# A macaron block with a spiking feed-forward: the first batch loaded and normalised in pieces, the last tiles' sums woven

## The chip, the cores and the metric

One core of a Trainium2 chip runs the whole program. The metric is the device time in microseconds of one execution; lower is better. Three runs of the kernel before gave 158.92 us in the median (158.81 to 158.99).

## What is computed

```python
x = x + 0.5 * ffn(layernorm(x), W_fc, W_proj)
x = x + attention(layernorm(x))
x = x + 0.5 * ffn(layernorm(x), W_fc, W_proj)

def ffn(x, W_fc, W_proj):                 # x: 8 batches, 512 tokens, 128 features; float32
    h = square(relu(x @ W_fc.T))          # 512 hidden features
    y = h @ W_proj.T
    # 5 steps of a leaky integrate-and-fire neuron driven by y: the number of spikes / 5
def attention(h):
    keys, values = h @ Wk.T + bk, h @ Wv.T + bv
    w = exp((keys @ Wka.T + bka) / sqrt(128))
    return cumsum(w / cumsum(w) * keys) * values
```

## The kernel before

The work is 16 feed-forward jobs (two layers of 8 batches) and 8 attention jobs in one software pipeline. Every engine runs the same loop over steps i from -3 to 18 and in each step issues its share of job i, of the jobs ahead (i+1, i+2) and behind (i-1, i-2, i-3); the order within a step is written out by hand, and semaphores tie the engines together. A batch is 512 tokens by 128 features, held as four tiles of 128 tokens (NT = 4). The eight PSUM banks are hidden[0] to hidden[3], work[0] and work[1] (one for each of two lanes, odd and even jobs), att_work and att_value.

A feed-forward job goes like this. VectorE takes BN_STATS and BN_AGGR of each tile (L488, L491) and reduces to var + eps and -mean (L497, L499); GpSimd raises var + eps to -0.5 (L330) and normalises four tiles (L338). TensorE turns them (transposes with the identity, L725) into work[lane]; ScalarE copies the bank to in_hi in the reduced float format of the matmul (L385), VectorE subtracts it from the bank to get the rest, in_lo (L522). An expand (L713, L714, L717) is three matmuls in one bank: fc_lo with in_hi, fc_hi with in_hi, fc_hi with in_lo; there are four, one for each 128 hidden features, and the first waits for in_lo only before its third matmul. ScalarE takes the relu (L389), squares are shared among ScalarE, VectorE and GpSimd, and four contracts (L760) sum y in work[lane]. The spikes are counted by comparing y with levels.

The first job differs: VectorE normalises it (first_normalise, L516), after GpSimd's inverse deviation alone. Its order on VectorE in step -1 is layer_norm of all four tiles, the cast of the identity to 16 bits (L622), first_normalise, then fc_low_part (L626), which makes fc_lo for all 512 columns from hidden[2], where the turned fc weights stand, and ScalarE's fc_hi (L448). In step 0 comes in_lo. TensorE starts with 14 transposes of the identity into hidden[0], results unused (fillers, L837), turns the fc weights (L840) and the projection weights (L844), issues 8 fillers (L847), turns the batch, issues 10 fillers (L867) and, after a wait for fc_lo, starts the first expand. ScalarE copies the turned projection weights (L450) right behind fc_hi.

SyncE issues the loads in this order: batch 0 as one load of 256 KB (L301), the projection weights (L302), batch 1, three attention weights, batch 2, five vectors, batches 3 to 7. ScalarE issues the fc weights (L381).

The last job ends tile by tile: TensorE contracts tile t into a bank of its own (L770, y_tiles) over hidden chunks c = 1 to 3, all three of tile 0 first, then of tile 1, and so on (chunk 0 of all tiles goes before; the matmul of one tile and chunk shows as two passes). ScalarE makes three 128-column steps of each tile (stairs, L403). VectorE (last_tiles) adds them in two operations (L541, L546) and adds the residual in a third (L550), each waiting for the one before, tile after tile. SyncE stores each tile (L316). Chunks 1 and 2 of the last job's squares are VectorE's (L534), 3 is ScalarE's.

Of the kernel before, what the change touches and what calls it, by code (L numbers as in the profile page):

```python
# [146 lines left out]
def macaron_kernel(nc, x, wk, bk, wka, bka, wv, bv, gamma, beta, w_fc, w_proj, out):  # L147
# [4 lines left out]
    HALF = S // 2  # L152
# [13 lines left out]
    WARM_UP, WARM_UP_TURN, WARM_UP_FIRST = 14, 8, 10  # L166
# [7 lines left out]
    with ExitStack() as ctx:  # L174
# [18 lines left out]
        att_work, att_value = bank("att_work"), bank("att_value")  # L193
        last_lane = (len(FF_JOBS) - 1) % 2
# [57 lines left out]
        x_loaded = [sem(f"x_loaded{b}") for b in range(NB)]  # L252
# [25 lines left out]
        sum_tile_made, x_tile_made = sem("sum_tile_made"), sem("x_tile_made")  # L278
# [42 lines left out]
        def _(pool):  # L321
# [6 lines left out]
            def normalise(kind, turn, source, by_dve=False):  # L328
# [3 lines left out]
                if by_dve:  # L332
                    return
# [7 lines left out]
            def ff_normalise(j):  # L341
                normalise(j.lane, j.turn, x_of[j.layer][j.batch], by_dve=j.index == 0)
# [37 lines left out]
        def _(act):  # L380
            act.dma_start(fc_raw[:], w_fc.rearrange("(c p) d -> p c d", p=P)).then_inc(fc_loaded, 16)  # L381

            def ff_hi(j):
                act.wait_ge(turned[j.lane], j.turn + 1)
                nc.scalar.activation(in_hi[j.lane][:], work[j.lane][:], ACT.Copy).then_inc(hi_made[j.lane], 1)  # L385
# [63 lines left out]
            act.wait_ge(proj_turned, 1)  # L449
            nc.scalar.activation(flat(proj_t), att_value[:], ACT.Copy).then_inc(proj_ready, 1)  # L450

            for i in range(FIRST_STEP, STEPS):
# [25 lines left out]
                for j in feed_forward(i + 1):  # L478
                    ff_hi(j)
                for b in attention(i + 1):  # L480
                    att_part_hi(b)
# [3 lines left out]
        def _(dve):  # L485
# [15 lines left out]

            def ff_layer_norm(j):
# [10 lines left out]
            def first_normalise(j):  # L513
                dve.wait_ge(rstd_made[j.lane], 1)
                for t in range(NT):
# [20 lines left out]

            def last_tiles(j):
                for t in range(NT):
                    tokens = slice(t * P, (t + 1) * P)
                    dve.wait_ge(sign_tile_made, 3 * t + 2)  # L540
                    nc.vector.scalar_tensor_tensor(sign_sum[j.lane][:, tokens], stairs[j.lane][:, 0, tokens], 2.0,  # L541
                                                   stairs[j.lane][:, 1, tokens], ALU.min,
                                                   ALU.add).then_inc(sum_tile_made, 1)
                    dve.wait_ge(sign_tile_made, 3 * t + 3)
                    dve.wait_ge(sum_tile_made, 2 * t + 1)
                    nc.vector.scalar_tensor_tensor(sign_sum[j.lane][:, tokens], stairs[j.lane][:, 2, tokens], 2.0,  # L546
                                                   sign_sum[j.lane][:, tokens], ALU.min,
                                                   ALU.add).then_inc(sum_tile_made, 1)
                    dve.wait_ge(sum_tile_made, 2 * t + 2)
                    nc.vector.scalar_tensor_tensor(x_of["out"][j.batch][:, t, :], sign_sum[j.lane][:, tokens],  # L550
                                                   RESIDUAL_STEP, x_of["second"][j.batch][:, t, :], ALU.mult,
                                                   ALU.add).then_inc(x_tile_made, 1)
# [71 lines left out]
            def fc_low_part():  # L624
                dve.wait_ge(fc_hi_made, 1)
                nc.vector.tensor_tensor(flat(fc_lo), hidden[2][:], flat(fc_hi).bitcast(F32),  # L626
# [31 lines left out]
            for i in range(FIRST_STEP, STEPS):  # L658
# [40 lines left out]
                if i == -1:  # L699
                    fc_low_part()  # L700
# [9 lines left out]
        def _(pe):  # L710
# [8 lines left out]
            def ff_turn(j):  # L719
# [3 lines left out]
                for t in range(NT):  # L723
                    pe.wait_ge(normed_made[j.lane], NT * j.turn + t + 1)
                    last = nc.tensor.transpose(work[j.lane][:, t * P:(t + 1) * P], normed[j.lane][:, t, :], ident[:])  # L725
                last.then_inc(turned[j.lane], 1)

            def ff_expand(j, c):
                if c == 0:
# [45 lines left out]
            def last_contract_tiles(j):  # L775
                for t in range(NT):
                    for c in range(1, NC):
                        if t == 0:
                            wait_square(j, c)
                        last_contract(j, t, c)  # L780
# [61 lines left out]
            pe.wait_ge(proj_loaded, 16)  # L842
            for c in range(NC):
                last = nc.tensor.transpose(att_value[:, c * P:(c + 1) * P], proj_raw[:, c, :], ident[:])  # L844
            last.then_inc(proj_turned, 1)
# [3 lines left out]
            for i in range(FIRST_STEP, STEPS):  # L849
                for j in feed_forward(i):  # L850
                    ff_turn(j)
                for j in feed_forward(i - 1):
# [75 lines left out]
```

## Time and profile before

| | us |
|---|---|
| median of 3 runs | 158.92 |
| the profiled execution | 158.94 |
| its span, first to last instruction | 157.2 |

| engine | busy us | share of span |
|---|---|---|
| TensorE (PE) | 150.6 | 96% |
| VectorE (DVE) | 135.1 | 86% |
| ScalarE (ACT) | 122.0 | 78% |
| GpSimd (POOL) | 109.4 | 70% |

PE's row counts pipelined matmuls with modelled ends, so 96% is not an engine at its peak; PEld is the loading of weights, which overlaps it. In the timeline a row is a run of equal instructions: start, length of the run, engine, line, operation, what is written and read, how many, and in brackets the engine's idle time before it and what ended it. In the chain a row is a piece of the path that ended last: each piece goes back to what released it. SPq and ACTq are DMA issues. Times are from the start of the span.

### The profile page before, as it was taken

The numbers are of one execution on the slowest core, as the hardware profiler recorded it, in microseconds if no ns is written. First come the engines' busy times: TensorE is split into PE (matmuls) and PEld (weight loads), VectorE is DVE, ScalarE is ACT, GpSimd is POOL, SyncE is SP. The second block draws the span as 40 slices with busy tenths as digits, with TensorE's granted clock in tenths as the row PEclk, the third lists the DMA queues.
The fourth block names the chain that finished last, engine by engine and source line by source line (L and its number), as shares of the span: only waits on it lengthen the run. The fifth ranks groups of instructions, "written<-read, shape, count | busy, mean of one in ns | idle before, by whom it ended". The sixth has DMA issues, their size and how long they took to land.

```text
span 157.2 us, 2605 instructions
## 1 busy us (share of the span) xinstructions
PE 150.6 (96%) x783; PEld 104.5 (66%) x783; DVE 135.1 (86%) x391; ACT 122.0 (78%) x237; POOL 109.4 (70%) x165
## 2 busy tenths in 40 slices
PE   6999999999999999999999999999999999999980
PEld 6685747585767858668566785775866758564870
DVE  1685499798899999999999999999999999875864
ACT  3348798999997894968989789598696786987970
POOL 1219427999699878799899999999987569270200
PEclk9999999999999999999999999999999999999997
DMA  4991000000000000000000020000020201020221
GB/s 127 260 284 47 0 2 4 0 0 0 2 2 4 0 0 2 0 4 0 0 0 0 4 67 2 0 0 0 2 71 0 67 0 54 13 73 0 67 83 53
DMA packets 10334, 5.08 MB, mean 32 GB/s; under 512 B 1104, under 2 KB 10192, under 8 KB 10320
## 3 DMA queue, kind: packets, MB, share of 16 engines
q1 hardware_dynamic: 9792, 4.66, 10.2%
q10 hardware_dynamic: 528, 0.26, 0.6%
q8 instruction: 6, 0.10, 0.2%
q14 instruction: 8, 0.07, 0.1%
HBM read 2.82 MB, written 2.10 MB: 31 GB/s over the span
## 4 chain that ended last, share of the span: by engine, by line
PE 89%; DVE 4%; DMA 2%; ACT 2%; POOL 1%; issue 0%; DVEq 0%
PE work L760 33%; PE hidden L713 9%; PE hidden L717 9%; PE hidden L714 9%; PE hidden L798 6%; PE work L725 5%; PE att_work L713 2%; PE att_work L717 2%; PE att_work L714 2%; DMA x_first<-_attn_hidden_states_dram 2%; PE att_work L807 2%; PE att_value L831 2%; PE att_value L713 1%; PE att_value L717 1%; PE att_value L714 1%; ACT stairs L418 1%
## 5 line engine op out<-in xcount | busy, mean ns | idle before, releaser
L760 PE MATMUL work<-square,proj_t 128*128 128x512 f32 x120 | 58.0, 595 | 0.0
L389 ACT ACTIVATE relu<-hidden 128x512 f32<-128x512 f32 x64 | 39.6, 621 | 13.2 <-PE hidden L717 13.1
L422 ACT ACTIVATE signs<-work 128x512 bf16<-128x512 f32 x70 | 41.2, 609 | 7.2 <-PE work L760 7.2
L394 ACT ACTIVATE square<-relu 128x512 f32<-128x512 f32 x45 | 29.5, 655 | 0.6
L330 POOL TENSOR_TENSOR rstd<-var_eps,minus_half 128x4 f32<-128x4 f32 x16 | 17.2, 1077 | 17.6 <-DVE neg_mean L499 17.6
L760 PEld LDWEIGHTS work<-square,proj_t 128*128 128x128 f32 x120 | 20.3, 189 | 12.7 <-issue 6.0
L598 DVE RECIPROCAL inv_sum<-weight_sum 128x256 f32<-128x256 f32 x16 | 27.9, 1741 | 0.0
L713 PE MATMUL hidden<-in_hi,fc_lo 128*128 128x512 f32 x64 | 27.0, 422 | 0.0
L717 PE MATMUL hidden<-in_lo,fc_hi 128*128 128x512 f32 x64 | 25.3, 396 | 0.0
L714 PE MATMUL hidden<-in_hi,fc_hi 128*128 128x512 f32 x64 | 25.0, 391 | 0.0
L338 POOL TENSOR_SCALAR normed_att<-x_att,neg_mean_att,rstd_att 128x128 f32<-128x128 f32 x32 | 18.9, 605 | 0.8
L360 POOL TENSOR_TENSOR share<-weight,inv_sum 128x256 f32<-128x256 f32 x16 | 13.3, 831 | 5.7 <-DVE inv_sum L598 5.7
L338 POOL TENSOR_SCALAR normed<-x_second,neg_mean,rstd 128x128 f32<-128x128 f32 x32 | 16.4, 528 | 0.8
L350 POOL TENSOR_TENSOR square<-relu 128x512 f32<-128x512 f32 x10 | 10.4, 1045 | 8.0 <-ACT relu L389 8.0
L522 DVE TENSOR_TENSOR in_lo<-work,in_hi 128x512 fp32r<-128x512 f32 x16 | 11.0, 686 | 5.7 <-ACT in_hi L385 5.5
L717 PEld LDWEIGHTS hidden<-in_lo,fc_hi 128*128 128x128 f32 x64 | 12.0, 188 | 3.0 <-DVE in_lo L522 0.3
L725 PEld LDWEIGHTS work<-ident,normed 128*128 128x128 f32 x64 | 8.0, 140 | 8.9 <-ACT signs L422 4.1
L714 PEld LDWEIGHTS hidden<-in_hi,fc_hi 128*128 128x128 f32 x64 | 12.1, 189 | 2.2 <-issue 0.2
L713 PEld LDWEIGHTS hidden<-in_hi,fc_lo 128*128 128x128 f32 x64 | 12.1, 188 | 2.1 <-issue 0.2
L338 POOL TENSOR_SCALAR normed<-x_first,neg_mean,rstd 128x128 f32<-128x128 f32 x28 | 12.8, 472 | 0.7
L798 PEld LDWEIGHTS hidden<-ident,signs 128*128 128x128 bf16 x160 | 9.6, 98 | 4.6 <-issue 4.6
L363 POOL TENSOR_TENSOR share_key<-share,key 128x256 f32<-128x256 f32 x16 | 11.7, 730 | 1.3
(103 smaller groups left out, 262.9 us busy)
## 6 DMA issues: line engine op xcount, KB each, us to landing
x_first<-_attn_hidden_states_dram SPq DMA_DIRECT2D x8, 256.0 KB, 4.0
out_dram<-x_out SPq DMA_DIRECT2D x7, 256.0 KB, 2.2
fc_raw<-in_L_ffn_W_fc_dram ACTq DMA_DIRECT2D x1, 256.0 KB, 4.1
proj_raw<-in_L_ffn_W_proj_dram SPq DMA_DIRECT2D x1, 256.0 KB, 4.2
out_dram<-x_out SPq DMA_DIRECT2D x4, 64.0 KB, 1.5
att_raw<-in_L_attn_Wk_dram SPq DMA_DIRECT2D x1, 64.0 KB, 3.9
att_raw<-in_L_attn_Wv_dram SPq DMA_DIRECT2D x1, 64.0 KB, 3.6
att_raw<-in_L_attn_Wka_dram SPq DMA_DIRECT2D x1, 64.0 KB, 3.5
```

The lines of the kernel that those rows point to most:

```text
L330: nc.gpsimd.tensor_tensor(rstd[kind][:], var_eps[kind][:], minus_half[:], ALU.pow).then_inc(rstd_made[kind], 1)
L338: nc.gpsimd.tensor_scalar(normed[kind][:, t, :], source[:, t, :], neg_mean[kind][:, t:t + 1], rstd[kind][:, t:t + 1], ALU.add, ALU.mult).t ...
L389: nc.scalar.activation(relu[j.lane][:, c, :], hidden[c][:], ACT.Relu).then_inc(relu_made[j.lane], 1)
L394: nc.scalar.activation(square[j.lane][:, c, :], relu[j.lane][:, c, :], ACT.Square).then_inc(squares_act[j.lane], 1)
L422: nc.scalar.activation(signs[j.lane][:, k, :], work[j.lane][:], ACT.Sign, bias=bias, scale=scale).then_inc(signs_made[j.lane], 1)
L598: nc.vector.reciprocal(inv_sum[:, cols], weight_sum[b % ATT_SETS][:, cols]).then_inc(inv_made, 1)
L713: nc.tensor.matmul(dst, w_lo, x_hi, start=True, stop=False)
L714: nc.tensor.matmul(dst, w_hi, x_hi, start=False, stop=False)
L717: return nc.tensor.matmul(dst, w_hi, x_lo, start=False, stop=True)
L725: last = nc.tensor.transpose(work[j.lane][:, t * P:(t + 1) * P], normed[j.lane][:, t, :], ident[:])
L760: mm = nc.tensor.matmul(work[j.lane][:], proj_t[:, c, :], square[j.lane][:, c, :], start=(c == CONTRACT_ORDER[0]), stop=(c == CONTRACT_ORD ...
L798: last = nc.tensor.matmul(count_bank[:, tokens], addend[:, tokens], ident16[:], start=(k == 0), stop=(k == len(addends) - 1))
```

## The change

The first batch comes in as four loads of one tile (64 KB) each, with a semaphore each. Its layer norm is done in halves of two tiles: first_layer_norm on VectorE for tiles 0 and 1, the identity's cast, the same for tiles 2 and 3; GpSimd takes the inverse deviation in two operations of two columns; VectorE then normalises the halves one after the other. The first half is turned into work[0], columns 0 to 255, the second into hidden[1], columns 256 to 511, and ScalarE's copy and VectorE's difference are made by half. fc_lo is made in two pieces: the first 128 columns, on which the first expand waits, and the other 384, on which the second waits; in_lo of the first half stands between them.

The projection weights' load moves from SyncE's queue to ScalarE's, behind the fc weights; their transposes move behind those of the first batch, and ScalarE's copy of them behind in_hi. The fillers become 14 (unchanged), 1 behind the fc weights, 3 between the halves, 2 before the first expand.

At the end TensorE's order of (tile, chunk) becomes (0,1), (1,1), (0,2), (0,3), (1,2), (1,3), then tiles 2 and 3 as before; VectorE issues the first sum of tile t, the residual of tile t-1, the second sum of tile t, with the first sums on a semaphore of their own.

```diff
-    WARM_UP, WARM_UP_TURN, WARM_UP_FIRST = 14, 8, 10
+    WARM_UP, WARM_UP_TURN, WARM_UP_HALF, WARM_UP_FIRST = 14, 1, 3, 2
...
+        first_second_half = hidden[1]
...
-            sp.dma_start(x_of["first"][0][:], x_tiles[0]).then_inc(x_loaded[0], 16)
-            sp.dma_start(proj_raw[:], w_proj.rearrange("d (c f) -> d c f", f=P)).then_inc(proj_loaded, 16)
+            for t in range(NT):
+                sp.dma_start(x_of["first"][0][:, t, :], x_tiles[0][:, t, :]).then_inc(first_tile_loaded[t], 16)
...
+            def first_inverse_deviation(j):
+                pool.wait_ge(first_args_made, 2)
+                nc.gpsimd.tensor_tensor(rstd[j.lane][:, 0:HALF_TILES], var_eps[j.lane][:, 0:HALF_TILES],
+                                        minus_half[:, 0:HALF_TILES], ALU.pow).then_inc(first_rstd_made, 1)
+                pool.wait_ge(ln_args_made[j.lane], 2)
+                nc.gpsimd.tensor_tensor(rstd[j.lane][:, HALF_TILES:NT], var_eps[j.lane][:, HALF_TILES:NT],
+                                        minus_half[:, HALF_TILES:NT], ALU.pow).then_inc(rstd_made[j.lane], 1)
...
             act.dma_start(fc_raw[:], w_fc.rearrange("(c p) d -> p c d", p=P)).then_inc(fc_loaded, 16)
+            act.dma_start(proj_raw[:], w_proj.rearrange("d (c f) -> d c f", f=P)).then_inc(proj_loaded, 16)
+
+            def first_hi(j):
+                act.wait_ge(first_turned, 1)
+                nc.scalar.activation(in_hi[j.lane][:, 0:HALF], work[j.lane][:, 0:HALF],
+                                     ACT.Copy).then_inc(first_hi_made, 1)
+                act.wait_ge(turned[j.lane], 1)
+                nc.scalar.activation(in_hi[j.lane][:, HALF:S], first_second_half[:, HALF:S],
+                                     ACT.Copy).then_inc(hi_made[j.lane], 1)
...
             def last_tiles(j):
                 for t in range(NT):
...
+                    last_first_pair(j, t)
+                    if t:
+                        last_add(j, t - 1)
+                    last_second_pair(j, t)
+                last_add(j, NT - 1)
...
                 for j in feed_forward(i + 1):
-                    ff_layer_norm(j)
                     if j.index == 0:
+                        first_layer_norm(j, 0)
                         fc_split_ident()
-                        first_normalise(j)
+                        first_layer_norm(j, 1)
+                        first_normalise(j, 0)
+                        first_normalise(j, 1)
+                        first_fc_low_part()
+                        first_half_lo(j)
+                        other_fc_low_parts()
+                    else:
+                        ff_layer_norm(j)
...
+                    bank_of = first_second_half if j.index == 0 and t >= HALF_TILES else work[j.lane]
+                    last = nc.tensor.transpose(bank_of[:, t * P:(t + 1) * P], normed[j.lane][:, t, :], ident[:])
+                    if j.index == 0 and t == HALF_TILES - 1:
+                        last.then_inc(first_turned, 1)
+                        for _ in range(WARM_UP_HALF):
+                            nc.tensor.transpose(hidden[0][:, 0:P], ident[:], ident[:])
...
             def ff_expand(j, c):
+                if j.index == 0 and c == 0:
+                    pe.wait_ge(first_hi_made, 1)
+                    pe.wait_ge(first_fc_ready, 1)
+                    pe.wait_ge(first_lo_made, 1)
+                if j.index == 0 and c == 1:
+                    pe.wait_ge(fc_ready, 1)
...
+                order = [(0, 1), (1, 1), (0, 2), (0, 3), (1, 2), (1, 3), (2, 1), (2, 2), (2, 3), (3, 1), (3, 2), (3, 3)]
...
                     ff_turn(j)
+                    if j.index == 0:
+                        turn_proj()
```

## Rows read from the trace of the kernel before

**Rows 1.** The page, part 4: shares of the chain by engine.
```profile
PE 89%; DVE 4%; DMA 2%; ACT 2%; POOL 1%; issue 0%; DVEq 0%
```

**Rows 2.** The chain of waits, first 20 us: start us, us, what.
```profile
0.72 3.66 DMA x_first<-_attn_hidden_states_dram
...
4.40 0.87 DVE stats L488 x4
...
5.89 1.04 POOL rstd L330
...
8.46 1.09 PE hidden L867 x10
```

**Rows 3.** The timeline of the first 17 us: start us, us, engine, instructions.
```profile
1.55 3.25 PE L837 MATMUL hidden<-ident 128*128 128x128 f32 x14 [1.55 <-POOL ident L325]
...
5.52 0.60 ACT L448 ACTIVATE fc_hi<-hidden 128x512 fp32r<-128x512 f32 x1 [3.02 <-PE hidden L840]
...
6.17 0.43 SPq L308 DMA_DIRECT2D vectors<-in_L_attn_beta_dram  x1
...
6.96 1.11 DVE L516 TENSOR_SCALAR normed<-x_first,neg_mean,rstd 128x128 f32<-128x128 f32 x4 [1.01 <-POOL rstd L330]
...
7.36 1.10 PE L725 MATMUL work<-ident,normed 128*128 128x128 f32 x4 [0.34 <-DVE normed L516]
...
8.50 0.60 ACT L385 ACTIVATE in_hi<-work 128x512 fp32r<-128x512 f32 x1 [1.72 <-PE work L725]
9.13 0.69 DVE L522 TENSOR_TENSOR in_lo<-work,in_hi 128x512 fp32r<-128x512 f32 x1 [0.45 <-ACT in_hi L385]
...
9.87 0.50 PE L717 MATMUL hidden<-in_lo,fc_hi 128*128 128x512 f32 x1
...
11.65 0.55 DVE L631 COPY att_t<-att_work 128x384 f32<-128x384 f32 x1
```

**Rows 4.** Windows: A:B, us, busy of five engines, PEclk, DMA share, GB/s.
```profile
1.50:3.00 1.50, 1.45 (x7) 1.45 (x8) 0.00 (x0) 1.00 (x1) 0.00 (x0) 1.00 0.51 127
3.00:4.80 1.80, 1.80 (x9) 1.39 (x7) 0.40 (x2) 0.00 (x0) 0.00 (x0) 1.00 1.09 357
```

**Rows 5.** DMA issues: what, queue, count, KB each, median us to landing.
```profile
out_dram<-x_out SPq DMA_DIRECT2D x4, 64.0 KB, 1.5
...
att_raw<-in_L_attn_Wka_dram SPq DMA_DIRECT2D x1, 64.0 KB, 3.5
...
vectors<-in_L_attn_beta_dram SPq DMA_DIRECT2D x1, 0.5 KB, 2.2
```

**Rows 6.** GpSimd's groups by form: busy us, mean ns of one, idle before.
```profile
L330 POOL TENSOR_TENSOR rstd<-var_eps,minus_half 128x4 f32<-128x4 f32 x16 | 17.2, 1077 | 17.6 <-DVE neg_mean L499 17.6
...
L323 POOL MEMSET minus_half<- 128x4 f32 x1 | 0.1, 103 | 0.0
```

**Rows 7.** The timeline of the last 17 us, TensorE and ScalarE.
```profile
149.84 0.52 PEld L770 LDWEIGHTS work<-proj_t,square 128*128 128x128 f32 x4 [0.27 <-DVE square L534]
...
150.60 0.61 ACT L403 ACTIVATE stairs<-work 128x128 uint8<-128x128 f32 x3 [0.96 <-PE work L770]
...
151.27 0.61 ACT L403 ACTIVATE stairs<-att_work 128x128 uint8<-128x128 f32 x3
```

**Rows 8.** The timeline of VectorE alone, from 150.5 us on.
```profile
151.07 0.29 DVE L541 SCALAR_TENSOR_TENSOR sign_sum<-stairs 128x128 bf16<-128x128 uint8 x1 [0.68 <-ACT stairs L403]
151.47 0.29 DVE L546 SCALAR_TENSOR_TENSOR sign_sum<-stairs,sign_sum 128x128 bf16<-128x128 uint8 x1
151.79 0.29 DVE L550 SCALAR_TENSOR_TENSOR x_out<-sign_sum,x_second 128x128 f32<-128x128 bf16 x1
152.00 0.28 DVE L541 SCALAR_TENSOR_TENSOR sign_sum<-stairs 128x128 bf16<-128x128 uint8 x1
152.74 0.29 DVE L546 SCALAR_TENSOR_TENSOR sign_sum<-stairs,sign_sum 128x128 bf16<-128x128 uint8 x1 [0.46 <-ACT stairs L403]
...
154.92 0.29 DVE L550 SCALAR_TENSOR_TENSOR x_out<-sign_sum,x_second 128x128 f32<-128x128 bf16 x1
```

More of the change, by code:

```diff
@@ L500, in layer_norm, with first_layer_norm @@
                                         negate=True).then_inc(ln_args_made[kind], 1)
+            def first_layer_norm(j, half):
+                tiles = range(half * HALF_TILES, (half + 1) * HALF_TILES)
+                of = slice(tiles[0], tiles[-1] + 1)
+                made = ln_args_made[j.lane] if half else first_args_made
+                for t in tiles:
+                    dve.wait_ge(first_tile_loaded[t], 16)
+                    nc.vector.bn_stats(stats[j.lane][:, t, :],
+                                       x_of[j.layer][j.batch][:, t, :]).then_inc(stats_made[j.lane], 1)
+                for t in tiles:
+                    dve.wait_ge(stats_made[j.lane], t + 1)
+                    nc.vector.bn_aggr(moments[j.lane][:, t, 0:2], stats[j.lane][:, t, :]).then_inc(moments_made[j.lane], 1)
+                dve.wait_ge(moments_made[j.lane], tiles[-1] + 1)
+                if half == 0:
+                    dve.wait_ge(consts_made, 1 + len(KINDS))
+                nc.vector.tensor_reduce(var_eps[j.lane][:, of], moments[j.lane][:, of, 1:3], AXIS.X,
+                                        ALU.add).then_inc(made, 1)
+                nc.vector.tensor_reduce(neg_mean[j.lane][:, of], moments[j.lane][:, of, 0:1], AXIS.X, ALU.add,
+                                        negate=True).then_inc(made, 1)
             def ff_layer_norm(j):
@@ L511, in att_layer_norm, with first_normalise @@
                 layer_norm("att", b, x_of["att"][b])
-            def first_normalise(j):
-                dve.wait_ge(rstd_made[j.lane], 1)
-                for t in range(NT):
+            def first_normalise(j, half):
+                dve.wait_ge(rstd_made[j.lane] if half else first_rstd_made, 1)
+                for t in range(half * HALF_TILES, (half + 1) * HALF_TILES):
                     nc.vector.tensor_scalar(normed[j.lane][:, t, :], x_of[j.layer][j.batch][:, t, :],
@@ L518, in first_normalise, with first_half_lo @@
                                             ALU.mult).then_inc(normed_made[j.lane], 1)
-            def ff_lo(j):
+            def first_half_lo(j):
+                dve.wait_ge(first_hi_made, 1)
+                nc.vector.tensor_tensor(in_lo[j.lane][:, 0:HALF], work[j.lane][:, 0:HALF],
+                                        in_hi[j.lane][:, 0:HALF].bitcast(F32),
+                                        ALU.subtract).then_inc(first_lo_made, 1)
+            def ff_lo(j):
+                if j.index == 0:
+                    dve.wait_ge(hi_made[j.lane], 1)
+                    nc.vector.tensor_tensor(in_lo[j.lane][:, HALF:S], first_second_half[:, HALF:S],
+                                            in_hi[j.lane][:, HALF:S].bitcast(F32),
+                                            ALU.subtract).then_inc(lo_made[j.lane], 1)
+                    return
                 dve.wait_ge(hi_made[j.lane], j.turn + 1)
@@ L622, in fc_split_ident, with first_fc_low_part, other_fc_low_parts @@
                 nc.vector.tensor_copy(ident16[:], ident[:]).then_inc(ident16_made, 1)
-            def fc_low_part():
+            def first_fc_low_part():
                 dve.wait_ge(fc_hi_made, 1)
-                nc.vector.tensor_tensor(flat(fc_lo), hidden[2][:], flat(fc_hi).bitcast(F32),
+                nc.vector.tensor_tensor(fc_lo[:, 0, :], hidden[2][:, 0:P], fc_hi[:, 0, :].bitcast(F32),
+                                        ALU.subtract).then_inc(first_fc_ready, 1)
+            def other_fc_low_parts():
+                nc.vector.tensor_tensor(flat(fc_lo)[:, P:FF], hidden[2][:, P:FF], flat(fc_hi)[:, P:FF].bitcast(F32),
                                         ALU.subtract).then_inc(fc_ready, 1)
@@ L775, in last_contract_tiles @@
             def last_contract_tiles(j):
[L776 to L780, printed above, removed]
+                order = [(0, 1), (1, 1), (0, 2), (0, 3), (1, 2), (1, 3), (2, 1), (2, 2), (2, 3), (3, 1), (3, 2), (3, 3)]
+                waited = set()
+                for t, c in order:
+                    if c not in waited:
+                        wait_square(j, c)
+                        waited.add(c)
+                    last_contract(j, t, c)
             def ff_count(j):
```

75 lines of the change are left out of this document (44 added, 31 removed).

## Prediction

> **What bounds the kernel now.** I read the chain of work that ended last first: 89% of it is TensorE [rows 1]. After 8.5 us it stays on TensorE until 145 us, so what lies ahead of the first matmul is paid once and shifts everything behind it, and what lies behind the last matmul is paid once more. The change touches just these two ends. The chain at the start [rows 2] goes from the load of the first batch (0.72 to 4.38) over VectorE's statistics of four tiles, GpSimd's inverse deviation (1.04 us) and VectorE's normalising to the transposes, the fillers of L867 and the first expand. The timeline at the start [rows 3] shows the same with what runs beside it. The anchor is L717, the third matmul of the first expand, at 9.87: it waits for in_lo (L522), and from it all of the first job follows. At the end, the view of VectorE alone [rows 8] shows twelve short operations in a row, 151.07 to 155.2, each waiting for the one before it; ScalarE is ready well ahead [rows 7].
>
> The profiled execution took 158.94 us with a span of 157.2, so 1.8 us lie outside the span; the median of the three runs is 158.92. The sum is made against 158.94.
>
> **Start: the load.** One load of 256 KB becomes four of 64 KB. SP's issues stand 0.495 us apart (the first load's at 0.72, beta's, eleven issues later, at 6.17 [rows 2, 3]), so tiles 0 to 3 are issued at 0.72, 1.21, 1.71 and 2.21. No row shows a 64 KB load on an empty queue. Below stands the 64 KB store's 1.5 us from issue to landing, above the 3.5 us of Wka, which queued behind other loads [rows 5]: tile 1 lands between 2.7 and 4.7, tile 3 between 3.7 and 5.7. Up to 3.0 us the engines moved only 127 GB/s, 190 KB, about three tiles; from 3.0 they moved 357 GB/s [rows 4]. The same bytes landed whole at 4.38. I take 3.3 for tile 1 and 4.3 for tile 3, near that row: the last tile gains nothing from the cut, the first two gain 1 us.
>
> The DMA rule that speaks against this part is in the Trainium skill, "DMA: Bandwidth & Descriptors", section Bandwidth: transfers under 64 KB are bound by descriptors, and it gives 0.95 us for 64 KB alone. Taken one after the other, four of these would last 3.8 us, as an estimate from that page, where 256 KB at the row's rate take under 1 us. Up to 3.0 us the trace does show a rate far from its best; no row shows pieces following each other.
>
> **Start: layer norm in halves.** From the landing (4.38) to GpSimd's start (5.89) went 1.51 for four tiles [rows 2]. With one tile already measured when the half's second lands, three statistics fall away, 0.2 each ((0.87 - 0.28) / 3, with 0.28 for one), and two of four aggregates, under 0.1 each: 0.8 is left. GpSimd starts on the first half at 3.3 + 0.8 = 4.1; for the second VectorE also casts the identity first, and it starts at 5.2.
>
> The inverse deviation of two columns in place of four has no row. The operation on four columns took 1.04 us in the chain [rows 2] and 1.08 in the mean; an operation with next to no arithmetic on the same shape 0.10 [rows 6]. If the duration above 0.10 goes with the columns, two cost 0.56; if it doesn't, 1.04. I take 0.8, half way, and keep 0.1 to 1.04. So the first ends at 4.9, the second at 5.2 + 0.8 = 6.0; with 1.04 the second ends at 6.2, with 0.56 at 5.8. Nothing else is queued on GpSimd until batch 1.
>
> The Trainium skill, "GPSIMD Engine Reference", section 2.1 Instruction dispatch, says that each core runs a software loop over the elements of its own 16 partitions, with some tens of cycles for dispatch. By that the duration would go with the columns, and the sum would gain 0.2 over mine; no row tells.
>
> **Start: what follows.** Before, normalising began 0.04 after GpSimd's end, its four operations 0.257 apart (1.11 for four of 0.34), TensorE's transposes of them 0.40 after each, ScalarE's copy 0.37 after the last transpose's start [rows 3]. First half: normalised at 5.1 and 5.36, transposed by 5.8, in_hi at 6.13, just when ScalarE is free from fc_hi (5.52 + 0.60 [rows 3]). That half is covered. Second half: normalised at 6.06 and 6.32, last transpose at 6.72, in_hi at 7.09; a copy of 256 columns I put at 0.39, between 0.60 for 512 [rows 3] and 0.28 for 128 (three in 0.61, 0.17 apart [rows 7]), end 7.48.
>
> VectorE is then the late one. Its queue behind the last normalising (6.32) starts at 6.57 with the first quarter of fc_lo, then in_lo of the first half, the rest of fc_lo, in_lo of the second. A 512-wide operation on a bank lasts 0.69, a 128-wide one 0.28, with the next 0.08 before its end [rows 3, 8]; by a straight line the four cost 0.21, 0.34, 0.47 and 0.42 to the end. So 6.57 + 1.44 = 8.01, and L717 0.05 later at 8.06 (before: 9.13 + 0.69 to 9.87). It was 9.87: **1.8 us earlier**. With GpSimd at 1.04 it is 8.29, a gain of 1.6; with 0.56, 7.82, a gain of 2.05; with 0.10, fc_hi (6.12) holds up fc_lo and the gain is 2.2. With tile 3 at 5.7 the gain is 0.4; at 3.7, 2.1. Copying the other three quarters of fc_lo ahead of the second in_lo costs 0.1, as in_hi is there at 7.5 and VectorE comes at 7.59; fc_lo is no longer a whole 0.69 ahead of everything.
>
> **Costed at nothing.** The projection weights: their issue (0.5) moves in front of ScalarE's table load, which has 3.02 us of idle time behind it [rows 3]. They share the second queue with fc_raw and land near 6; their transposes (four, 0.109 apart, the spacing of L867's ten [rows 2]) run at 6.9 to 7.3 while TensorE waits for in_hi, and the copy (0.6) fills ScalarE from 7.5 to 8.1, before the first relu at 8.6. If the load came after 7.5, its wait would stand ahead of the first expand on TensorE and cost what it is late. SP: three more issues for tiles and one less for the weights move all later loads by two issues, 1.0 us. The last vector was issued at 6.17, now 7.15, and with the 2.2 us that it took [rows 5] lands at 9.4. It is wanted by the attention weights' copy, at 11.65 before and 9.85 now [rows 3]: 0.4 of margin, and what waits there is batch 2's statistics, which are not late. Batch 1, issued at 2.7, is wanted right behind in_lo at 8.0; with the first load's 3.66 and the 1.0 of queue it lands at 7.4. Two banks for two halves: hidden[1] is free until the second expand, which comes behind L717.
>
> **End.** On TensorE tile 1's first product (two passes, 0.22) moves into the wait for VectorE's square (0.27 idle [rows 7]). Tile 0 stays, tiles 1 to 3 come 0.22 sooner. ScalarE's three steps take 0.61 and start 0.67 apart per tile (150.60, 151.27 [rows 7]), behind TensorE; tile 3's last step ends at 153.0 for 153.2. On VectorE a dependent operation started 0.40 after the first sum's start and 0.32 after the second's, an independent one 0.21 (151.07, 151.47, 151.79, 152.00 [rows 8]). Before, a tile cost 0.40 + 0.32 + 0.21 = 0.92. Woven, the next tile's first sum stands between: second sum, +0.21 first sum of the next, +0.21 residual, +0.21 second sum: 0.63 per tile. From 151.47: second sums at 152.10, 152.73, 153.36, the last residual at 153.69. ScalarE's steps are there 0.07 or more ahead of each. It was 154.92: **1.2 us earlier**. Of it 0.35 is a hole in tile 1 (152.00 to 152.74 where 0.40 is usual [rows 8]), which the steps do not explain; if it returns, the gain is 0.9. If even the waits of the independent ones shrink, 1.4. The four stores are then issued 0.63 apart, above SP's 0.495, and each lands after 1.5 [rows 5].
>
> **Sum.** 158.94 - 1.8 - 1.2 = 155.9. Ends: 158.94 - 2.3 - 1.4 = 155.2; 158.94 - 0.6 - 0.9 = 157.4.
>
> **Rivals.** (a) The pieces are late: tile 3 takes as long as Wka's load and lands at 5.7. The head gains 0.4, in all 157.3. For: four starts; against: the engines were at 127 GB/s and had room. 10%. (b) The clock drops for a while. Of TensorE's fillers 6 are left of 18 after the weights. In the first 3.3 us 14 of its transposes took 3.25, later 10 took 1.09 [rows 2, 3], 0.23 each for 0.11: the first is 1.2 GHz, the second 2.4 GHz, though the granted clock's column says 1.00 for both stretches [rows 4]. Real work and fillers from 4.8 to 8.1 are 18 x 0.109 = 2.0 us, 60%, for 73% before. If the clock fell to 1.2 GHz at about 8 us and stayed there as long as at first, 3.3 us, half of this is lost: 157.6. 8%. (c) The same with a longer stretch is the case on the other side: it decides from 6 us at 1.2 GHz, where half of it equals the 3.0 gained; with 7.5 us the time is 159.7. Against it: so long a stretch with TensorE at work lies nowhere in the trace. 4%. (d) The head's gain is lost in the middle, another engine being what TensorE follows: 157.7. Against it: behind the loads nothing is tied to absolute time, all engines shift. 5%. (e) The gain doesn't come at all because a load or the projection's wait holds the first expand as long as before while the hole returns: about 158.9, 3%.
>
> **How the numbers follow.** Forecast 155.9 with 70%. The range of 155.2 to 157.4 takes in the forecast and (a), 80%. About 0.2% is what a measurement of this kernel can tell from no change. Faster 93%, the same 3%, slower 4%.
>
> **What would show it.** First BN_STATS at about 2.9 to 3.3, the two inverse deviations at 4.1 and 5.2 with 0.6 to 1.0 each, L717 at 8.1, the last residual 1.2 nearer to the last y tile, twelve short operations 0.21 apart in place of 0.32 to 0.40. Wrong if tile 3's statistics start after 4.8, if matmuls of the first job stand at twice their spacing, or if L717's gain isn't found again at the last job's first matmul.

## The result

The changed kernel took 156.96 us in the median of 12 runs (156.84 to 158.59), the kernel before 158.91 (158.68 to 159.15, 12 runs): ratio 0.9886, 95% interval 0.9872 to 0.9899. That is 1.95 us or 1.2% faster. 155.9 was predicted, 3.0 us faster, with a range of 155.2 to 157.4. The profiled execution took 156.96 with a span of 155.2.

The timeline of the changed kernel's first 10 us:

```profile
0.71 0.46 ACTq L395 DMA_DIRECT2D fc_raw<-in_L_ffn_W_fc_dram  x1
0.72 1.81 SPq L307 DMA_DIRECT2D x_first<-_attn_hidden_states_dram  x4
...
3.24 0.29 DVE L538 BATCH_NORM_STATS2 stats<-x_first 128x6 f32<-128x128 f32 x1 [1.77 <-DMA x_first<-_attn_hidden_states_dram]
4.21 0.29 DVE L538 BATCH_NORM_STATS2 stats<-x_first 128x6 f32<-128x128 f32 x1 [0.68 <-DMA x_first<-_attn_hidden_states_dram]
...
4.59 1.02 PE L942 MATMUL hidden<-ident,fc_raw 128*128 128x128 f32 x4
...
5.03 0.48 DVE L538 BATCH_NORM_STATS2 stats<-x_first 128x6 f32<-128x128 f32 x2
5.06 0.72 POOL L335 TENSOR_TENSOR rstd<-var_eps,minus_half 128x2 f32<-128x2 f32 x1 [3.57 <-DVE neg_mean L548]
...
5.65 0.60 ACT L474 ACTIVATE fc_hi<-hidden 128x512 fp32r<-128x512 f32 x1 [2.60 <-PE hidden L942]
...
6.06 0.73 POOL L338 TENSOR_TENSOR rstd<-var_eps,minus_half 128x2 f32<-128x2 f32 x1 [0.28 <-DVE neg_mean L548]
...
6.83 0.60 DVE L565 TENSOR_SCALAR normed<-x_first,neg_mean,rstd 128x128 f32<-128x128 f32 x2 [0.34 <-POOL rstd L338]
...
7.22 0.40 PEld L809 LDWEIGHTS hidden<-ident,normed 128*128 128x128 f32 x2 [0.26 <-DVE normed L565]
...
7.85 0.39 ACT L403 ACTIVATE in_hi<-hidden 128x256 fp32r<-128x256 f32 x1 [0.55 <-PE hidden L809]
...
8.38 0.47 PE L796 MATMUL hidden<-in_hi,fc_lo 128*128 128x512 f32 x1
...
8.81 0.19 PEld L800 LDWEIGHTS hidden<-in_lo,fc_hi 128*128 128x128 f32 x1 [0.16 <-DVE in_lo L578]
8.92 0.40 PE L800 MATMUL hidden<-in_lo,fc_hi 128*128 128x512 f32 x1
```

The first inverse deviation starts at 5.06 in place of 5.89 [rows 2] and the second at 6.06. The first expand's third matmul (now L800) stands at 8.92 in place of 9.87 [rows 3]: the start gained 0.95. The chain goes over the load of tile 1, to 4.19, from there over VectorE without a stop to 6.25, and then over TensorE. As printed it passes TensorE's fillers between the halves; the rows show that the second half's transposes waited for VectorE (7.22), whose normalising had waited for the second inverse deviation.

VectorE alone at the end of the changed kernel:

```profile
150.05 0.29 DVE L601 SCALAR_TENSOR_TENSOR sign_sum<-stairs 128x128 bf16<-128x128 uint8 x1 [0.68 <-ACT stairs L429]
150.80 0.29 DVE L609 SCALAR_TENSOR_TENSOR sign_sum<-stairs,sign_sum 128x128 bf16<-128x128 uint8 x1 [0.46 <-ACT stairs L429]
151.00 0.28 DVE L601 SCALAR_TENSOR_TENSOR sign_sum<-stairs 128x128 bf16<-128x128 uint8 x1
151.21 0.28 DVE L616 SCALAR_TENSOR_TENSOR x_out<-sign_sum,x_second 128x128 f32<-128x128 bf16 x1
151.41 0.28 DVE L609 SCALAR_TENSOR_TENSOR sign_sum<-stairs,sign_sum 128x128 bf16<-128x128 uint8 x1
...
152.62 0.29 DVE L609 SCALAR_TENSOR_TENSOR sign_sum<-stairs,sign_sum 128x128 bf16<-128x128 uint8 x1
152.94 0.29 DVE L616 SCALAR_TENSOR_TENSOR x_out<-sign_sum,x_second 128x128 f32<-128x128 bf16 x1
```

The first sum stands 1.02 earlier than before (150.05 for 151.07 [rows 8]), so the start's gain has come through the middle whole. From the first sum to the last residual it took 3.85 before and takes 2.89 now: the end gained 0.96. The operations stand 0.20 to 0.21 apart, but for two: the last residual comes 0.32 behind the sum that it waits for, and 0.75 lie between the first tile's two sums where 0.40 is usual. The pause of 0.35, at tile 1 before [rows 8], is back, at another place. 0.95 and 0.96 make 1.9 of the 1.98 between the two profiled executions.

### The profile page after: what moved, and what is told of

It reads as the page before. It is cut to its first block, busy times and chain, and to the rows that moved or that the text cites. A ratio compares the mean times of both kernels' runs of the same rounds, so it can differ in the third digit from the quotient of the medians.

```text
span 155.2 us, 2591 instructions
## 1 busy us (share of the span) xinstructions
PE 149.2 (96%) x771; PEld 103.6 (67%) x771; DVE 135.0 (87%) x395; ACT 122.2 (79%) x238; POOL 108.8 (70%) x166
## 4 chain that ended last, share of the span: by engine, by line
PE 93%; DVE 2%; DMA 2%; ACT 0%; issue 0%; SPq 0%; ACTq 0%
PE work L860 33%; PE hidden L796 10%; PE hidden L800 10%; PE hidden L797 9%; PE hidden L900 7%; PE work L809 5%; PE att_work L796 2%; PE att_work L800 2%; PE att_work L797 2%; PE att_work L909 2%; PE att_value L933 2%; DMA x_first<-_attn_hidden_states_dram 2%; PE att_value L796 1%; PE att_value L800 1%; PE att_value L797 1%; PE work L870 1%
## 5 line engine op out<-in xcount | busy, mean ns | idle before, releaser
L796 PE MATMUL hidden<-in_hi,fc_lo 128*128 128x512 f32 x64 | 27.1, 423 | 0.0
L343 POOL TENSOR_TENSOR rstd<-var_eps,minus_half 128x4 f32<-128x4 f32 x15 | 16.2, 1080 | 13.3 <-DVE neg_mean L529 13.3
L800 PE MATMUL hidden<-in_lo,fc_hi 128*128 128x512 f32 x64 | 25.2, 393 | 0.0
L349 POOL TENSOR_SCALAR normed<-x_second,neg_mean,rstd 128x128 f32<-128x128 f32 x32 | 15.6, 497 | 0.8
L364 POOL TENSOR_TENSOR square<-relu 128x512 f32<-128x512 f32 x10 | 10.4, 1037 | 8.0 <-ACT relu L415 8.0
L583 DVE TENSOR_TENSOR in_lo<-work,in_hi 128x512 fp32r<-128x512 f32 x15 | 10.3, 686 | 5.1 <-ACT in_hi L411 5.1
L800 PEld LDWEIGHTS hidden<-in_lo,fc_hi 128*128 128x128 f32 x64 | 12.0, 188 | 2.9 <-DVE in_lo L578 0.2
L796 PEld LDWEIGHTS hidden<-in_hi,fc_lo 128*128 128x128 f32 x64 | 12.1, 188 | 2.1 <-issue 0.2
```

The lines of the kernel that those rows point to most:

```text
L343: nc.gpsimd.tensor_tensor(rstd[kind][:], var_eps[kind][:], minus_half[:], ALU.pow).then_inc(rstd_made[kind], 1)
L349: nc.gpsimd.tensor_scalar(normed[kind][:, t, :], source[:, t, :], neg_mean[kind][:, t:t + 1], rstd[kind][:, t:t + 1], ALU.add, ALU.mult).t ...
L796: nc.tensor.matmul(dst, w_lo, x_hi, start=True, stop=False)
L800: return nc.tensor.matmul(dst, w_hi, x_lo, start=False, stop=True)
```

## Experiments

### The two ends apart, and the pause

> The kernel before with the two edits of the end alone (TensorE's order of tile and chunk, VectorE's woven sums). The start is untouched. If the two ends add up, this gives the end's share alone: 0.95 us, 158.0. In the trace of the changed kernel the pause of 0.35 us ahead of a second sum was still there, at VectorE's 447th instruction as before. Theory A (the pause belongs to a place in VectorE's instruction stream, 128 instructions apart, the earlier ones at the 63rd and 191st): here too it stands at the 447th instruction, which is now the second sum of tile 1. Theory B (it is tied to stores or to waits of the last tiles): it stands at the first tile's second sum, as in the changed kernel, or is gone.

> The changed kernel with the end of the kernel before. If the two ends add up, 1.0 us faster than before: 157.9, with the third matmul of the first expand at 8.9 and the last job's first matmul 1.0 earlier. If the middle swallows the start's gain, 158.5 or more. Theory A puts the pause at the second sum of tile 0, theory B leaves it at tile 1.

The edits are the change's own, each half of the diff alone. Measured: the end alone 157.95 (ratio 0.9941, 0.9924 to 0.9957), the start alone 157.88 (0.9948, 0.9927 to 0.9969). 0.99 and 1.06 add up to 2.05, the whole gives 1.95: within the intervals the ends add up. The profiled execution of the start alone took 158.43, with the third matmul at 9.51 and not at 8.9; the clock at its start comes up again below. VectorE's last operations, first of the end alone, then of the start alone:

```profile
151.41 0.29 DVE L548 SCALAR_TENSOR_TENSOR sign_sum<-stairs,sign_sum 128x128 bf16<-128x128 uint8 x1
151.62 0.28 DVE L540 SCALAR_TENSOR_TENSOR sign_sum<-stairs 128x128 bf16<-128x128 uint8 x1
151.82 0.28 DVE L555 SCALAR_TENSOR_TENSOR x_out<-sign_sum,x_second 128x128 f32<-128x128 bf16 x1
152.35 0.29 DVE L548 SCALAR_TENSOR_TENSOR sign_sum<-stairs,sign_sum 128x128 bf16<-128x128 uint8 x1 [0.25 <-ACT stairs L403]
```

```profile
150.57 0.29 DVE L602 SCALAR_TENSOR_TENSOR sign_sum<-stairs 128x128 bf16<-128x128 uint8 x1 [0.68 <-ACT stairs L429]
151.31 0.29 DVE L607 SCALAR_TENSOR_TENSOR sign_sum<-stairs,sign_sum 128x128 bf16<-128x128 uint8 x1 [0.46 <-ACT stairs L429]
151.64 0.29 DVE L611 SCALAR_TENSOR_TENSOR x_out<-sign_sum,x_second 128x128 f32<-128x128 bf16 x1
```

The pause stands at tile 1's second sum in the first, at tile 0's in the second. In both, in the kernel before and in the changed one this is the 447th record of VectorE's stream, counted from 0 and with its semaphore instructions. The releaser named in brackets was done long before. Theory B falls; the last test of A moves the stream by two (of the edit the lines that issue them):

```diff
             nc.vector.memset(ones[:], 1.0).then_inc(consts_made, 1)
+            for k in range(2):
+                nc.vector.memset(pad[:, k:k + 1], 0.0).then_inc(pad_made, 1)
```

> The changed kernel with two more memsets of one column each at VectorE's start, where it is idle until the first tile lands; nothing else. Theory A: the 447th instruction is now the first sum of tile 0, ahead of which VectorE waits 0.7 us for ScalarE anyway, so the pause is hidden and the kernel is 0.3 to 0.35 us faster than the changed one: 156.6. Theory B: no change, 156.96.

```profile
151.38 0.29 DVE L602 SCALAR_TENSOR_TENSOR sign_sum<-stairs 128x128 bf16<-128x128 uint8 x1 [0.68 <-ACT stairs L430]
151.77 0.29 DVE L610 SCALAR_TENSOR_TENSOR sign_sum<-stairs,sign_sum 128x128 bf16<-128x128 uint8 x1
...
153.91 0.29 DVE L617 SCALAR_TENSOR_TENSOR x_out<-sign_sum,x_second 128x128 f32<-128x128 bf16 x1
```

The pause is gone: 0.39 between the first two sums, and 2.53 from the first sum to the last residual in place of 2.89. That is the 0.36 of theory A. The time, 156.83 (three runs of 156.74 to 156.88, one of 157.94), is only 0.1 below the changed kernel, not 0.3 (the three other than 157.94 lie about 0.2 below it). In its profile 143.74 lie between the third matmul and the last residual, for 144.02 in the changed kernel, so 0.28 of the 0.36 is there; where the rest went I can't say, since the profiled execution is the one of 157.94, which differs in its start. That run shows something else, its TensorE at the start:

```profile
8.88 0.64 PE L970 MATMUL hidden<-ident 128*128 128x128 f32 x2
9.17 0.78 PE L799 MATMUL hidden<-in_hi,fc_lo 128*128 128x512 f32 x1
9.74 0.63 PE L800 MATMUL hidden<-in_hi,fc_hi 128*128 128x512 f32 x1
10.17 0.55 PE L803 MATMUL hidden<-in_lo,fc_hi 128*128 128x512 f32 x1
10.55 0.40 PE L799 MATMUL hidden<-in_hi,fc_lo 128*128 128x512 f32 x1
```

The first expand's matmuls take 0.78 and 0.63 where 0.47 and 0.40 are usual, and the two fillers before them stand 0.21 apart. The trace's record of the granted clock starts the 2.4 GHz at 10.49 in this execution, 4.83 in the profile of before and 5.44 in that of the changed kernel. The third matmul stands at 10.17, 1.25 later than in the changed kernel, and the execution took 1.1 longer than the other three.

> The changed kernel with TensorE's old order of tile and chunk, the woven sums kept. The reorder brought tiles 1 to 3 forward by 0.22 us. VectorE's last operations run 0.6 apart per tile and start 0.35 late because of the pause, so ScalarE's steps are not what they wait for at the last tile unless they come under 0.1 late: I expect 0.0 to 0.2 us slower than the changed kernel, 156.96 to 157.15. If the reorder carries the end's gain, 157.4 or more.

```diff
-                order = [(0, 1), (1, 1), (0, 2), (0, 3), (1, 2), (1, 3), (2, 1), (2, 2), (2, 3), (3, 1), (3, 2), (3, 3)]
...
+                for t in range(NT):
+                    for c in range(1, NC):
+                        if t == 0:
+                            wait_square(j, c)
+                        last_contract(j, t, c)
```

Measured 156.94 for 156.96. ScalarE's steps of tile 3 start 2.01 after those of tile 0 (149.52 to 151.53) with the old order and 1.78 (149.57 to 151.35) with the new, so the reorder does bring them forward by 0.23, and nothing waits for them. The end's gain is the weave's alone. That the pause hides what the reorder would give is possible; no run had the old order without the pause.

### Which load is late

> The changed kernel with the projection weights' load back on SyncE's queue, behind the four tiles. In the changed kernel tile 3 landed at 5.16 us, not at 4.3, while both weights' loads on ScalarE's queue were in by 4.8. Theory C (ScalarE's queue takes the larger share of the DMA engines, and the tiles wait until it is empty): with only the fc weights on it, tile 3 lands at 4.6 to 4.7, the third matmul of the first expand comes 0.5 earlier, 156.45. Rival D (small loads are slow by themselves, whatever the other queue does): tile 3 stays at 5.1 to 5.2, 156.95.

```diff
...
-            act.dma_start(proj_raw[:], w_proj.rearrange("d (c f) -> d c f", f=P)).then_inc(proj_loaded, 16)
+            sp.dma_start(proj_raw[:], w_proj.rearrange("d (c f) -> d c f", f=P)).then_inc(proj_loaded, 16)
```

156.95, no change; the tiles took 2.4 to 3.0 us from issue to landing, for 2.5 to 3.3, and tile 3 was in at 5.04. Theory C misses: the projection weights are not what holds up the tiles.

> The changed kernel with both weights' loads on SyncE's queue behind the four tiles; ScalarE issues nothing. Theory C: tile 3 lands at 4.0 to 4.2, the fc weights at 4.8 to 5.2; the turned fc weights and ScalarE's copies of them (to 6.7) are then what the first expand waits for, its third matmul at 8.2, 156.2. Rival D: tile 3 at 5.1, no gain, and the fc weights 1 us later may cost something: 157 or more.

The edit moves both lines to SyncE, behind the tiles. How long the loads took from issue to landing, the tiles of the changed kernel, and the tiles and the fc weights of this one:

```profile
DMA to landing us min/median/max: 2.5/3.0/3.3
```

```profile
L307 SPq DMA_DIRECT2D x_first<-_attn_hidden_states_dram x4: 382/422/437, 0.7 to 2.1; - x4
...
DMA to landing us min/median/max: 1.8/1.9/2.0
```

```profile
L308 SPq DMA_DIRECT2D fc_raw<-in_L_ffn_W_fc_dram x1: 434/434/434, 2.6 to 2.6; - x1
...
  PEld hidden L942: 1.7, 1
  PE hidden L942: 1.3, 1
...
DMA to landing us min/median/max: 3.5/3.5/3.5
```

With nothing on the other queue tile 1 is measured at 3.17 and tile 3 lands 1.9 after its issue at 2.1, so at 4.0: these are the 3.3 and 4.3 of the prediction, and rival D falls. But the fc weights land at 6.1, TensorE waits 1.3 for them, and the time is 156.84 (156.59 to 158.04), the changed kernel's within the intervals and not theory C's 156.2. The profile is of the slowest of its six runs, 158.04: the third matmul stands at 10.05 and the clock rose at 9.11, both behind the landings read here. It is the fc weights' load that the tiles meet, not the projection weights', and one of the two is late in either order.

> The changed kernel with one wait more: ScalarE issues its two loads only when the identity is made (1.5 us in place of 0.7). Theory C: the tiles have the engines to themselves for 0.8 us longer, tile 1 at 3.4 to 3.8 and tile 3 at 4.6 in place of 5.16, the fc weights at 4.8; 156.4 to 156.6. Rival D: tile 3 stays, 156.95.

```diff
+            act.wait_ge(ident_made, 1)
             act.dma_start(fc_raw[:], w_fc.rearrange("(c p) d -> p c d", p=P)).then_inc(fc_loaded, 16)
```

157.91 (157.45 to 158.85), slower than the changed kernel by 1 us; both theories expected otherwise. VectorE's first statistics, and the second inverse deviation:

```profile
3.06 0.29 DVE L539 BATCH_NORM_STATS2 stats<-x_first 128x6 f32<-128x128 f32 x1 [0.29 <-DMA x_first<-_attn_hidden_states_dram]
...
4.89 0.29 DVE L539 BATCH_NORM_STATS2 stats<-x_first 128x6 f32<-128x128 f32 x1 [0.94 <-DMA x_first<-_attn_hidden_states_dram]
6.07 0.29 DVE L539 BATCH_NORM_STATS2 stats<-x_first 128x6 f32<-128x128 f32 x1 [0.89 <-DMA x_first<-_attn_hidden_states_dram]
...
6.91 0.73 POOL L338 TENSOR_TENSOR rstd<-var_eps,minus_half 128x2 f32<-128x2 f32 x1 [2.29 <-DVE neg_mean L549]
```

Tiles 0 and 1, issued ahead of the fc weights (1.53), are in by 3.06. Tiles 2 and 3, issued 0.1 and 0.55 behind them, wait for them: measured at 4.89 and 6.07. A small load just behind a large one on the other queue took about 3.3 us here (tile 2), and 4.0 (tile 3) with the projection weights, issued at 2.01, ahead of it as well.

> The changed kernel with batch 0 in one load of 256 KB, as before the change; the layer norm still in halves, all else as changed. What the cut into tiles is worth by itself. Theory C: the whole load shares the engines with both weights on ScalarE's queue and lands at 4.6 to 4.8 for all tiles; the second half then starts as early as with tiles or earlier, the first 0.5 later, and GpSimd's two inverse deviations follow each other: third matmul at 8.9 to 9.1, 156.95 to 157.15. Rival D: one large load is faster than four small ones, lands at 4.4, and the kernel is 0.3 faster than the changed one: 156.65.

157.43 (157.18 to 157.44 and one of 158.35): the cut is worth about 0.5, and both theories missed (156.95 to 157.15, and 156.65). The whole batch landed 3.5 after its issue, at 4.19, 1 us ahead of the changed kernel's tile 3 and together with its tile 1. So of the four tiles the cut brought one forward, tile 0 by 1.0 (3.22), left tile 1 where it was and held up tiles 2 and 3 by 0.8 and 1.0 (4.98 and 5.16). The fc weights landed at 4.55, for 4.01. The inverse deviations start at 5.25 and 6.24, for 5.06 and 6.06. That is 0.19 of the 0.47; the profile is of the run of 158.35, where the clock rose at 10.44, and what made the rest stays open. So tile 3's landing is not what counts when it comes within 1 us of tile 1's. From tile 1's landing to the second inverse deviation go 1.87 us of VectorE's queue in three kernels (4.19 to 6.06 in the changed one, 4.08 to 5.95 with the projection weights on SyncE, 3.15 to 5.02 with all weights there).

> The changed kernel with tiles 1 and 3 loaded by ScalarE's queue ahead of the fc weights, tiles 0 and 2 by SyncE's, the projection weights behind them on SyncE's. So all tiles are issued by 1.2 us, before the fc weights (1.7). With the fc weights' issue moved among the tiles, each load landed roughly in the order in which it was issued over both queues, and a load of 256 KB took 3.3 to 3.5 us from its issue. Theory E (order of issue over both queues decides): all four tiles land by 3.5, the fc weights at 5.0 to 5.2; the copies of the fc weights are then late, not the tiles, the third matmul of the first expand stands at 8.3 to 8.5 in place of 8.92, 156.4 to 156.6. Rival F (SyncE's queue loses whatever is on the other): tile 2 is late as before, 5.0, and nothing is gained: 156.9 or more.

```diff
...
+            for t in (1, 3):
+                act.dma_start(x_of["first"][0][:, t, :], x_tiles[0][:, t, :]).then_inc(first_tile_loaded[t], 16)
             act.dma_start(fc_raw[:], w_fc.rearrange("(c p) d -> p c d", p=P)).then_inc(fc_loaded, 16)
```

157.51; three of six runs took 156.78 to 157.0, three 158.02 to 159.04, and the profiled one is the slowest. In it all tiles were in by 3.9, where theory E had 3.5, and the fc weights at 6.7, 1.5 later than it had them. Rival F falls too, tile 2 being in at 3.7, though its time, 156.9 or more, is what came. TensorE stood idle up to 6.7, and the clock rose at 10.58.

> The tiles over two queues once more, ahead of the fc weights, but the projection weights behind the fc weights on ScalarE's queue, where they were in the changed kernel; the two memsets on VectorE; 16 fillers at the start in place of 14. In the run with the projection weights issued just ahead of the fc weights, tiles landed by 3.9 and the fc weights at 6.7, too late for TensorE, whose clock rose only at 10.6. Theory E (what lies ahead in the order of issue over both queues decides): with only the tiles ahead of them the fc weights land at 5.0 to 5.3, all tiles by 3.9, the third matmul of the first expand stands at 8.4 to 8.6, and with the pause hidden the kernel takes 156.3 to 156.5. Theory G (a load of 256 KB behind four small ones is late whatever is between): the fc weights land after 5.8 again, the kernel takes 156.8 or more with runs at 158.

The edit against the changed kernel is the one above, with the projection weights behind the fc weights, two memsets, and 16 for 14 fillers. 157.64 (156.76 to 158.67). One of its fastest executions (156.85) is the profiled one:

```profile
3.85 0.72 POOL L336 TENSOR_TENSOR rstd<-var_eps,minus_half 128x2 f32<-128x2 f32 x1 [2.36 <-DVE neg_mean L551]
...
6.16 0.66 PE L947 MATMUL hidden<-ident,fc_raw 128*128 128x128 f32 x4 [1.15 <-DMA fc_raw<-in_L_ffn_W_fc_dram]
...
7.48 0.29 DVE L703 TENSOR_TENSOR fc_lo<-hidden,fc_hi 128x128 fp32r<-128x128 f32 x1 [1.26 <-ACT fc_hi L477]
...
9.03 0.51 PE L805 MATMUL hidden<-in_lo,fc_hi 128*128 128x512 f32 x1
```

The first inverse deviation is 1.2 earlier than in the changed kernel, and all of it is lost to the fc weights, in at 6.1: the third matmul stands at 9.03. Theory E misses, and theory G's numbers came, but its reason isn't shown: with the projection weights off SyncE's queue batch 1's load of 256 KB stands there in their place, issued at 1.63 like the fc weights and landed at 5.73. No run has the fc weights behind the tiles on two queues with nothing else beside them. Between its first sum and its last residual lie 2.54 us, the pause hidden as in the kernel with two memsets.

### More fillers, and all together

> The changed kernel with four fillers behind the fc weights' transposes in place of one; at 0.21 us each they end at 6.3 at the latest, just when the first tile is turned. In the profiles with the old fillers the clock rose at 4.8 and 5.9 us; with the new ones at 5.4, 6.5, 6.7, 7.5, 9.1, 10.4 and 10.5, and the runs in which it rose after the first expand's start took 1 us more. If the thinner filling is what lets it rise late, the median stays at 156.96 (0.0 to 0.1 more) and slow runs become rarer or go away. If not, they stay at 1 in 10 to 1 in 4.

157.05 (156.79 to 157.14, 4 runs). None of four took 1 us more, which a rate of 1 in 12 gives anyhow: it tells nothing of the fillers. In its profile the clock rose at 7.51 and the third matmul stands at 9.09.

> Loads over two queues as in the first of these runs, the two memsets on VectorE and four fillers, together. If each does what it should and they add, 0.4 (loads) + 0.2 (the pause hidden, as measured): 156.3, the fastest so far. If the fc weights' later landing eats the loads' gain, 156.8.

158.5 (156.74 to 160.3, 12 runs): it doesn't add. As in the first kernel with two queues the projection weights were issued ahead of the fc weights. Three in four of its runs took 157.9 or more; four fillers didn't help in a kernel whose TensorE waits for a load up to 5.9.

## Why the prediction was right, and where it was off

The direction, the range and both mechanisms were right; 1.1 of the 3.0 us were not there, 0.85 at the start and 0.25 at the end.

**The load** is the term that was off. "3.3 for tile 1 and 4.3 for tile 3" measured 4.19 and 5.16 in the changed kernel, and "the last tile gains nothing from the cut, the first two gain 1 us" failed too: only tile 0 gained, and tile 3 lost 1 us against the same batch in one load. The prediction's own sign of being wrong, tile 3's statistics after 4.8, came true: they started at 5.23. There was room on the engines up to 3.0 (127 GB/s [rows 4], 185 in the changed kernel), but the fc weights' load shared it: it landed at 4.01, where it took until 4.78 before, while tile 1 came 0.9 later than forecast. With it out of the way the two terms come out as predicted (3.15 and 4.0), and then it is itself late. Rival (a), with tile 3 at 5.7, had the right direction: six tenths of its delay were there.

The ends of the range took 2.3 and 0.6 for the start where the working beside them gives 2.2 and 0.4; the result lies clear of both.

Two rules of the Trainium skill can be held against this, both in "DMA: Bandwidth & Descriptors". The one of the section Bandwidth gives 0.95 us for a load of 64 KB that GpSimd issues; the prediction's estimate that four of them would follow each other at that distance is not borne out: alone on the engines the tiles landed 0.3 to 0.65 apart. The one of the section "Queues, rings and completion order", that each DMA engine takes turns between the queues it has work for, I had not weighed; the tiles' 1.9 us alone against 3.0 beside the fc weights agree with it.

**Layer norm in halves.** The 0.8 from a tile's landing to GpSimd's start measured 0.87 (4.19 to 5.06), and 0.90 for the second. I had not seen that VectorE's queue alone puts the second inverse deviation 1.87 behind tile 1's landing; with tile 1 at 3.3 both ways give the 5.2 of the prediction. **The inverse deviation** of two columns took 0.72 and 0.73, for 0.8 taken and bounds of 0.10 and 1.04. With 1.04 for four columns [rows 2] a straight line gives 0.16 a column and 0.40 fixed, as an estimate. The Trainium skill's "GPSIMD Engine Reference", section 2.1, by which the time goes with the elements behind a short dispatch, is half right here: 0.56 as the prediction worked it out, 0.72 measured.

**What follows**: from the end of the second inverse deviation to the third matmul 2.06 were predicted (6.0 to 8.06) and 2.13 measured (6.79 to 8.92). The prediction's path, over VectorE's in_lo, and the expand's own first two matmuls came out 0.11 apart. The weights made from in_lo (ready at 8.76) were loaded at 8.81, but the matmul came at 8.92: L796 started at 8.38, 0.14 behind in_hi's end, and 0.54 lie between it and L800. What was costed at nothing cost nothing: the projection weights landed at 4.8 and were wanted at 7.54, and ScalarE's copy of them ended at 8.9, ahead of the relu at 9.35. That the start's gain goes through the middle (against rival (d)) is shown by 0.95 at L800, 1.03 at the last job's first matmul (144.30 for 145.33) and 1.02 at the first sum.

**The end**: 0.96 for 1.2; the prediction gave 0.9 for the case that the hole returns, and it did. The 0.63 per tile measured 0.60 to 0.61. The reorder, costed with 0.22 for tiles 1 to 3, moved ScalarE by that and the time by nothing.

**Rival (b)**, a clock that falls at 8 us, was put at 1.7 us and 8%. What is there is not a fall but a rise that comes late, in some executions. 1 of 12 of the changed kernel took 158.59, 1.6 more than the others, which is not profiled; in the kernels with the new start whose profiled run took 1 us more the clock rose at 10.4 to 10.6 (two memsets, one load, the first two-queue kernel) or at 9.11 (the weights on SyncE's queue). A rise at 7.5 is among the fast ones: the old order's profile, of 156.90, has it at 7.53. It is not the only cause of such runs: the start alone was profiled in an execution of 158.43, where the clock rose at 6.5 and tile 1 landed at 4.8, 0.6 later than in the changed kernel. Of 12 runs of the kernel before none was off by over 0.3. That the thinner filling is the cause is argued from this, not shown: it wasn't varied with enough runs, and the share of such runs was largest where TensorE waited for a late load (9 of 12 with all together). The median hides it.

## What to carry to other kernels

When a load is cut up so that its first piece comes early, look at what is issued within a microsecond of it on any queue, and count the bytes that all have to be in before the first real work: here batch and fc weights, 512 KB. With the batch in one load both were in by 4.6 to 4.8 us; in four tiles the first came 1 us sooner, and the later of the two landed at 5.0 to 6.7 in every order of issue. The cut still paid, by about 0.5, of which 0.19 is explained. Dependent short operations on VectorE stand 0.32 to 0.40 apart and independent ones 0.20; weaving another tile's operations between them is worth the difference for each. Twelve filling matmuls fewer at the start showed no cost in the median, though no run left them out alone; look at all the runs, not at the median.

## What the runs showed of the hardware

VectorE paused for about 0.35 us at the 447th record of its instruction stream, in the kernel before, the changed one and the two halves of the change, at three different operations; two more instructions ahead of it moved it under a wait, and it was gone. Pauses of the same kind show at the 63rd record (0.36, a sum at 20.12 in the changed kernel) and at the 191st (about 0.25, in_lo at 58.93 before), which fit steps of 128. They do not show at every such place: record 63 of the kernel before stands 0.20 behind the one ahead, as its neighbours do, and record 319 shows none in either.

The trace has a sign of what it is. Among its DMA records are loads of the kind "instruction", of 8 KB each, eight within the span of every profiled execution. The last of them starts 0.66 to 0.81 us behind record 447 in all eleven kernels with the pause (151.50 in the changed one), and 2.4 to 2.7 ahead of that record in the three with the two memsets, where VectorE waits for ScalarE just ahead of that record. So the pause goes with a change of block in the instruction stream; that the change makes it is inferred. The Trainium skill, "Advanced Engine Details and Errata", section ISA Cache, has a cache line of 256 instructions; 447 and 191 are 256 apart, but 191 and 63 are 128.

A load of 64 KB took 1.8 to 2.0 us from issue to landing with nothing on the other queue, 2.4 to 3.3 beside a load of 256 KB issued at the same time, and up to 4.0 right behind one. A load of 256 KB took 3.2 to 3.6 at best, 3.7 to 4.2 where three were issued within 0.5 us on two queues (the kernel before), and 4.5 and 5.0 behind the tiles with another of 256 KB issued at the same time.
